# A chain of four graph layers on one core: the roots, scales and normalising moved by one or two tiles, and GpSimd's mask bias moved forward

## What is computed

```python
h1 = relu(adj @ (f1[:, None] * (adj @ (x @ W1))))                # layer 0
x = layernorm(x + adj @ (f2[:, None] * (adj @ (h1 @ W2))))
cos = beta * (x @ x.T) / (norm(x) @ norm(x).T + 1e-7)             # layer 1
x = layernorm(x + softmax(cos + (1 - adj) * -1e9, axis=1) @ x)
msg = relu((adj @ x) @ W_msg.T + b_msg)                           # layer 2
x = layernorm(x + gru_cell(msg, x))
x = layernorm(x + x @ W_self + (adj @ x / max(rowsum(adj), 1)) @ W_neigh)  # layer 3
```

## Time and profile before

| | us |
|---|---|
| median of 3 runs | 1708.02 |
| lowest and highest | 1703.11, 1709.55 |
| the profiled execution | 1705.44 |
| its span, first to last instruction | 1703.6 |
| TensorE busy in the span | 1646.8 (97%) |
| VectorE, ScalarE, GpSimd busy | 1376.6, 1235.0, 235.4 |

### The profile page before, as it was taken

How to read it: one execution, slowest core, us unless ns; L and a number is a source line. 1 busy time by engine, 2 the same in 40 slices (tenths; PEclk the granted TensorE clock), 3 DMA queues, 4 the chain that set the end, 5 groups by cost and what they waited for, 6 DMA issues and landing times.

```text
span 1703.6 us, 22249 instructions
## 1 busy us (share of the span) xinstructions
PE 1646.8 (97%) x8530; PEld 1374.7 (81%) x8530; DVE 1376.6 (81%) x1518; ACT 1235.0 (72%) x1251; POOL 235.4 (14%) x258
## 2 busy tenths in 40 slices
PE   7999999999999999988999999999999999999996
PEld 5878888888888888767999999999888767767885
DVE  6888888688778887786787888878888887787897
ACT  6776767677666766777777877877858777676775
POOL 0000000000000000148333333333330000000000
PEclk9999999999999999989999999999999999999998
DMA  9999999799989998982334444333569957858995
GB/s 377 384 364 360 376 338 385 281 385 355 354 300 376 368 367 291 330 333 81 129 138 149 149 149 149 141 129 133 212 227 354 349 176 247 292 163 289 342 344 175
DMA packets 63136, 461.61 MB, mean 271 GB/s; under 512 B 6672, under 2 KB 10928, under 8 KB 11312
## 3 DMA queue, kind: packets, MB, share of 16 engines
q1 hardware_dynamic: 63024, 460.14, 73.0%
HBM read 458.00 MB, written 2.11 MB: 270 GB/s over the span
## 4 chain that ended last, share of the span: by engine, by line
PE 82%; DVE 7%; ACT 4%; DMA 4%; issue 2%; POOL 2%; DVEq 0%; SPq 0%; ACTq 0%; POOLq 0%
PE ps L1194 17%; PE ps L1188 17%; PE ps L1185 17%; PE ps L1277 6%; DMA raw<-adjT 4%; DVE aL L804 4%; PE ps L1292 3%; PE ps L1294 3%; PE ps L1293 3%; PE ps L1262 3%; PE ps L1264 3%; PE ps L1263 3%; ACT aH L491 3%; PE ps L1224 1%; PE ps L1371 1%
## 5 line engine op out<-in xcount | busy, mean ns | idle before, releaser
L804 DVE TENSOR_TENSOR aL<-raw,aH 128x2048 fp32r<-128x2048 f32 (+1 forms) x364 | 826.0, 2274 | 179.8 <-ACT aH L491 178.5
L491 ACT ACTIVATE aH<-raw 128x2048 fp32r<-128x2048 f32 (+1 forms) x364 | 690.2, 1899 | 266.6 <-PE ps L1188 170.6
L1185 PE MATMUL ps<-aH,yH 128*128 128x512 f32 x1472 | 408.8, 400 | 13.3 <-ACT aH L491 13.2
L1194 PE MATMUL ps<-aL,yH 128*128 128x512 f32 x1472 | 399.9, 394 | 11.7 <-DVE aL L804 11.7
L1188 PE MATMUL ps<-aH,yL 128*128 128x512 f32 x1472 | 395.7, 391 | 0.0
L1194 PEld LDWEIGHTS ps<-aL,yH 128*128 128x128 f32 x1472 | 272.9, 188 | 82.9 <-DVE aL L804 28.0
L1185 PEld LDWEIGHTS ps<-aH,yH 128*128 128x128 f32 x1472 | 271.4, 189 | 77.9 <-issue 19.2
L1188 PEld LDWEIGHTS ps<-aH,yL 128*128 128x128 f32 x1472 | 276.8, 188 | 58.6
L986 DVE TENSOR_TENSOR ptL<-ps,ptH 128x512 fp32r<-128x512 f32 x256 | 176.6, 690 | 76.9 <-ACT ptH L627 74.2
L627 ACT ACTIVATE ptH<-ps 128x512 fp32r<-128x512 f32 x192 | 114.4, 596 | 101.8 <-PE ps L1277 96.8
L1292 PE MATMUL ps<-ptH,yH 128*128 128x256 f32 x512 | 145.5, 284 | 9.4 <-DVE ptL L986 8.6
(11 more groups left out here) (150 smaller groups left out, 1691.1 us busy)
## 6 DMA issues: line engine op xcount, KB each, us to landing
raw<-adjT SPq DMA_DIRECT2D x364, 1024.0 KB, 6.1
raw<-adj SPq DMA_DIRECT2D x28, 2048.0 KB, 7.9
raw<-adj SPq DMA_DIRECT2D x4, 1024.0 KB, 6.9
kept<-adj SPq DMA_DIRECT2D x2, 2048.0 KB, 14.9
kept<-adjT SPq DMA_DIRECT2D x4, 1024.0 KB, 12.5
xT<-norms SPq DMA_DIRECT2D x1, 2048.0 KB, 6.9
out<-xrow SPq DMA_DIRECT2D x8, 256.0 KB, 4.7
xrow<-x_rows SPq DMA_DIRECT2D x1, 1024.0 KB, 15.0
```

What stands on the lines that cost most here:

```text
L491: ins = nc.scalar.activation(a_tiles(q, t)[0][:, cols], a_source(q, t)[:, cols], ACT.Copy)
L804: ins = dve.tensor_tensor(low[:, cols], a_source(q, t)[:, cols], high.bitcast(F32)[:, cols], ALU.subtract)
L1185: pe.matmul(b, block(yH, k), high[:, c], start=(k == 0), stop=False)
L1194: ins = pe.matmul(b, block(yH, k), low[:, c], start=False, stop=(k == NB - 1))
```

## The change

In pass 3's second half the first root goes from u = 11 to u = 12 and steps 3 to 7 from u = 12 to u = 13; the unit rows go one tile later, and with them the turn, unitH and unitL. In the GRU the root goes one tile later, steps 3 to 7 one tile later, the two normalisings two tiles later, the high and low parts two tiles later, and of the turns and own shares those of the last two chunks of each half one tile later. On GpSimd the two mask biases of the second row of super block 1 go forward: the first to right behind the staging of that row, the second behind the next normalising; the last normalising of chunk 7 goes behind the low parts of chunks 4 and 5. No instruction is added or taken away in the source, and no transfer is moved.

```diff
--- before.py
+++ after.py
@@ -57,10 +57,10 @@
     X_LOADS = ((0, 1), (1, HBK), (HBK, BK))
     GRU_AT = ((2, 5, 8, 11), (0, 2, 4, 6))
     NORM_AT = ((11, 17), (8, 12))
-    HIGH_AT = ((15, 16, 21, 22), (12, 13, 16, 17))
-    TURN_AT = (18, 20, 23, 25)
-    SELF_AT = (20, 22, 25, 27)
-    UNIT_AT, X1_AT = (14, 16, 19, 21), (25, 27)
+    HIGH_AT = ((17, 18, 23, 24), (14, 15, 18, 19))
+    TURN_AT = (18, 20, 24, 26)
+    SELF_AT = (20, 22, 26, 28)
+    UNIT_AT, X1_AT = (15, 17, 20, 22), (25, 27)
     X2_LOW_AT = {4: 5, 5: 7, 6: 17, 7: 18}
     EARLY_TILES, FILL_FROM = 4, 6
     EARLY_HIGH = {1: (0, 0), 2: (0, 1), 4: (1, 0), 6: (1, 1), 8: (2, 0), 9: (2, 1), 12: (3, 0), 13: (3, 1)}
@@ -451,13 +451,14 @@
             normalise(1, HBK + 1)
             low_of_x(4, X1_BY_ACT + 1)
             stage_unit(1, 1)
+            mask_bias(1, 1, 0, 7)
             normalise(1, HBK + 2)
+            mask_bias(1, 1, 1, 8)
+            low_of_x(4, HBK)
+            low_of_x(4, HBK + 1)
             normalise(1, HBK + 3)
-            for c in range(HBK, BK):
-                low_of_x(4, c)
-                if c == HBK + 1:
-                    for h in range(2):
-                        mask_bias(1, 1, h, 7 + h)
+            low_of_x(4, HBK + 2)
+            low_of_x(4, HBK + 3)
 
             for sbi in range(2, NSB):
                 for r in range(2):
@@ -581,7 +582,7 @@
                     if q < 3 and u >= 6 and (u - 6) % BPB == 0 and (u - 6) // BPB < HBK:
                         high_of_filtered(q, (u - 6) // BPB)
                     if q == 3:
-                        if u == 11:
+                        if u == 12:
                             root(0, 0, NB // 2)
                         for c in range(HBK):
                             if u == UNIT_AT[c]:
@@ -725,10 +726,10 @@
                     if u == GRU_AT[h][i] + 3:
                         gates(c)
                 for g in range(2):
-                    if u == NORM_AT[h][g]:
+                    if u == NORM_AT[h][g] + 1:
                         root(4 + 2 * h + g, (h * HBK + 2 * g) * BPB, (h * HBK + 2 * g + 2) * BPB)
-                    if u in (NORM_AT[h][g] + 2, NORM_AT[h][g] + 3):
-                        c = h * HBK + 2 * g + u - NORM_AT[h][g] - 2
+                    if u in (NORM_AT[h][g] + 4, NORM_AT[h][g] + 5):
+                        c = h * HBK + 2 * g + u - NORM_AT[h][g] - 4
                         act.wait_ge(rstd_ready, 5 + 2 * h + g)
                         normalise(c, x_by_act)
                 for i in range(HBK):
@@ -915,7 +916,7 @@
                         if u == 10:
                             for i in range(3):
                                 scale_step(i, 0, HBK, 0, NB // 2)
-                        if u == 12:
+                        if u == 13:
                             for i in range(3, SCALE_STEPS):
                                 scale_step(i, 0, HBK, 0, NB // 2)
                         for c in range(HBK):
@@ -1095,7 +1096,7 @@
                     if u == NORM_AT[h][g] - 1:
                         for i in range(3):
                             scale_step(i, 4 + 2 * h + g, value, lo, hi)
-                    if u == NORM_AT[h][g] + 1:
+                    if u == NORM_AT[h][g] + 2:
                         for i in range(3, SCALE_STEPS):
                             scale_step(i, 4 + 2 * h + g, value, lo, hi)
```

## The result

The changed kernel takes 1701.24 us (median of 12 runs, 1696.32 to 1706.67) against 1707.36 us of the kernel before (12 runs, 1701.81 to 1712.34). The ratio is 0.9968 with an interval of [0.9955, 0.9982]: 5.5 us faster, within the 0.5% named in the prediction. The forecast was 1702.1 us. The prediction took 0.5% for the least that can be told from no change; with twelve runs of each kernel the interval leaves out 1, so these 0.3% can be told.

A forecast was written before the change was run, and what follows sets the result against it. TensorE, busy 97% of the span, was taken as the bound, so only its idle time (some 22 us here) could be won. -3.1 + 1.2 - 2.8 - 1.2 = -5.9 us; from the 1708.0 median, 1702.1 us, range 1694.5 to 1708.5.

The forecast's parts named there:

- A: Attention start: GpSimd's new order ends VectorE's 4.94 us wait for the mask bias; -3.1 us, bounds -5.5 and 0.
- B: Pass 3's second half: later steps and units lose time; +1.2 us (0.2 + 1.0), bounds -1 to +2.5.
- C: GRU's first half: 3.0 us lost instead of 5.8; -2.8 us, bounds -4.6 and 0.
- D: GRU's second half: 5.0 us lost instead of 6.2; -1.2 us, bounds -5.0 and +1.
- the five steps: Scale steps moved one tile later: 1.2 to 1.3 us lost at pass 3's u = 14, 1.1 at GRU second half's u = 11.
- the pair: Pass 3, u = 25: normalising chunk 0 and the last unitH copy share a tile; 1.7 us plus some 0.4, singly 1.1.
- Term A's clock: Attention start: clock falls behind 4.04 us idle, not behind 2.55; at 1.9 us idle the fall was taken as gone.
- The hole: Attention start: TensorE's weight load idle 4.04 us up to 793.38, predicted to shrink to some 1.9 us.
- Rival 3: Attention: TensorE idles nearer 4 us, clock stays low ten us; +5 instead of -3.1, sum +2.2, 1710.2 us; chance 0.07.
- the root's wait: GRU's first half: root waited 1.57 us for VectorE, holding u = 18's split; one tile later the variance is ready.
- Rival 1: More won: wait for chunk 7 hidden (-5.5 in attention), both saved table loads count (2.6); sum -10.9, 1697.1 us; chance 0.22.
- Rival 2: VectorE gives it back: GRU first half -1, second +0.5, sum -2.4, 1705.6 us; chance 0.2.

The follow-up runs named there:

- e2_pass3_only: Kernel before with only pass 3's root, scale steps and units one tile later; pass 3 from u = 10 took 68.9 us for 67.7, attention 497.3.
- e3_gru_only: Kernel before with only the GRU's part of the change; GRU halves took 50.3 and 66.7 us for 53.4 and 67.4.
- e1_bias_only: Kernel before with only GpSimd's new order; attention took 494.9 us for 497.2.
- e8_units_only: Kernel before with only pass 3's unit rows one tile later; pass 3 from u = 10 took 68.8 us for 67.7.
- e6_root_at_8: Changed kernel with the first group's root and scale steps in the GRU's second half back at u = 8 and 9; that stretch took 66.4 us for 66.3.
- e5_x1_at_24: Changed kernel with chunk 0 of x normalised at u = 24 of pass 3 for u = 25; pass 3 from u = 10 took 67.6 us for 69.0.
- e10_gru_roots_back: Changed kernel with all GRU roots and scale steps one tile back; GRU halves took 50.8 and 66.0 us for 50.3 and 66.3.
- e4_chunk7_sooner: Changed kernel with GpSimd normalising chunk 7 before the low parts and the second bias half; attention took 491.8 us for 494.4.

## Why the prediction was right, and where it wasn't

**The sum.** -5.9 us predicted, -5.8 by the stretches, 0.9968 by the runs. Term by term it is A -3.1 for -2.8, B +1.2 for +1.3, C -2.8 for -3.1, D -1.2 for -1.1, so the sum owes little to errors that cancel (0.3 us in A against 0.3 in C). Alone, B gives +1.2 (e2_pass3_only), C and D together -3.9 (e3_gru_only), and A -2.3 (e1_bias_only), the weakest of the three. What made it work is that each queue was followed in order from the rows' own durations, tile by tile, and that what is late next was asked at each removed wait: chunk 7 in attention, the five steps at u = 14 and u = 11, the pair at u = 25. All of these are in the trace after, with 3.33 us for "about 3", 1.27 for "1.2 to 1.3", 1.69 for 1.7, and 1.1 lost by u = 11 (3.80 us for 2.72) for 1.1.

**Term A's clock** was the step that failed. Idle time under 2.55 us was taken for safe; behind this very idle time the clock fell in e3_gru_only and e8_units_only, and behind 2.68 us in e6_root_at_8. More than half of the 2.8 us is there because the clock fell behind the hole in the profile before and did not in the one after, and by the other profiles both can come out otherwise (1.7 us between the means). That -3.1 met -2.8 so closely is in this part luck. The hole itself was sized too short, 2.41 us of the weight queue for 1.9. The sum still held because a fall is cheap at this place, 0.8 to 1.6 us. Rival 3 supposed ten us of it; the second fall was 3.4 us long in each of the five profiles that had one.

**Term B** priced the pair at 1.0 us over the singles. By e8_units_only that is right, but e5_x1_at_24 gets 1.4 back, so one of the old order's losses wasn't needed either: with the unitH copy at u = 24 and normalising at u = 25, u = 25 and 26 lost 0.62 + 0.49 us before; with normalising first (u = 24) and the copy at u = 25 they lose 0.07 + 0.45.

**Term C** was sized well for a reason that was half right. The prediction named three things: the low part of x and chunk 1's normalising, which leave, and the root's wait, which goes when it stands one tile later. e10_gru_roots_back shows 2.7 of 3.1 us without the last of them. u = 20 came nearly as priced (4.99 us against 4.2 to 4.3 without a loss, so 0.7 to 0.8 for 0.85); the 0.3 that the term was short lie at u = 17, which lost 0.6 us where I left 0.95.

**Term D** said the loads saved count nothing here, as they stand where TensorE is waited for. For the first one that holds. The second isn't hidden in e6_root_at_8: that kernel gets 2.0 us back at u = 11 and 12 and loses 2.4 at u = 13 to 15, behind a load that the changed kernel doesn't have. The prediction took the losses from u = 13 on as gone, which they are (13.7 us for u = 13 to 17, for 16.9 before), and laid all of it to the distance of the steps. But fewer loads are no gain by themselves: e10_gru_roots_back has all three and takes 66.0 us for the 66.3 with one. Rival 1, in so far as it counted both loads as 2.6 us, was too high. The Trainium skill, ScalarE: Activation LUTs, section Rules for kernel authors, asks to do all of one table set before switching; by the rows here that is worth one load's length, 1.28 us, at most, and e10_gru_roots_back, which doesn't follow it, is 0.3 us faster. The Trainium skill, ScalarE: Activation LUTs, section What ACT_TABLE_LOAD costs, gives 1.38 us of drain to each switch beside the load itself; it shows in none of these rows, neither before the load at 1519.34 (the tanh before it ends at 1519.32) nor behind it, where the root starts at 1520.64, 1.30 us after the load does, and at 1523.65 behind the load at 1522.35.

**Rival 1's other half**, that the wait for chunk 7 could be hidden, is true of another order (e4_chunk7_sooner), not of this one. **Rival 2** (VectorE gives it back) is out: it needed C at -1. The upper end of the range, 1708.5, isn't reached by the words given for it (halfway from rival 2 to rival 3 is 1707.9); nothing hangs on it.

## What to carry to other kernels

Where work is placed by hand in strictly ordered queues, cost a move by replaying the few tiles around it from the trace's own durations, and at each wait that goes, ask which semaphore is the next late one; that gave each term here to 0.3 us, though in term A with luck in the clock. Two steps of which the first waits for another engine's end of tile should not share a tile, and an engine with a long fixed list should be ordered by who waits for each item (chunk 7, for which ScalarE stood 3.33 us, came behind two low parts that could wait, as e4_chunk7_sooner shows). Compare stretches and not spans, when the part of the time before the change scatters more than the change is worth, and look at more than one profile of a stretch whose clock can fall.

## What was not expected of the hardware

- TensorE's clock fell behind an idle weight queue of 2.55 us in two executions and did not in the ten others that had the same idle time at the same place; behind 2.68 us it fell, behind 2.71 it did not. The low stretch behind it was 3.4 us each time; the one that began within attention's first idle time (6.4 us between matmuls) was 6.8 or 10.2 us, without an effect on the stretch's length that could be told.
- The time up to pass 3's u = 10 varied by 11 us between executions whose instructions are the same up to there, by single tiles that were loaded late. The sum of ScalarE's waits for them (38.9 to 111.6 us) follows it only loosely. The four stretches of the changed kernel repeated within 0.1 us in its two profiles, and the time behind them differed by 0.7.
